# Top-2 mixture FFN behind a quantised linear block: experts chosen from token sums, and a first pair of column tiles without Strassen sums

## The reference

```python
x = x + xattn(layernorm(x), gate_up_weight, down_weight)   # per batch: int8-style linear 512 -> 512, silu(gate) * up, linear 256 -> 512
x = x + ffn(layernorm(x), gate_w, w1, b1, w2, b2)

def ffn(hidden, gate_w, w1, b1, w2, b2):                     # 8 experts, DFF = 2048
    x = hidden.reshape(-1, d)
    router_logits = x @ gate_w.T
    _, sel = top_k(router_logits.sum(axis=0), 2)             # one choice of two experts for all 2048 rows
    rw = softmax(router_logits[:, sel], axis=1)
    h = gelu(einsum('nd,kdf->knf', x, w1[sel]) + b1[sel])
    y = einsum('knf,kfd->knd', h, w2[sel]) + b2[sel]
    return einsum('nk,knd->nd', rw, y)
```

## Time and profile before

| | |
|---|---|
| median of 3 runs | 849.64 us (849.06 to 851.92) |
| the profiled execution | 847.23 us, span 845.4 us |
| TensorE | 772.4 us busy, 3569 matmuls |
| VectorE | 487.1 us, 695 instructions |
| GpSimd | 458.6 us, 463 instructions |
| ScalarE | 365.1 us, 675 instructions |
| DMA | 32.31 MB, mean 38 GB/s |

### The profile page before, as it was taken

The page is one execution under the profiler, slowest core; times in us unless marked ns, Lnnn a source line. Parts: engine busy times, 40 slices in busy tenths (PEclk is TensorE's granted clock), DMA queues, the critical chain, the costliest instruction groups (busy, mean ns, idle before and its releaser), DMA issues.

```text
span 845.4 us, 11484 instructions
## 1 busy us (share of the span) xinstructions
PE 772.4 (91%) x3569; PEld 620.1 (73%) x3575; DVE 487.1 (58%) x695; ACT 365.1 (43%) x675; POOL 458.6 (54%) x463
## 2 busy tenths in 40 slices
PE   3687766649999999999999999999999999999998
PEld 2564553337888888888888888888888888888886
DVE  2999999597545454545545454545454545454545
ACT  7975565653333343434333333333333334343422
POOL 1567779674645455555555555555454545464622
PEclk9799889869999999999999999999999999999999
DMA  8400000030101010101010101010101000000023
GB/s 340 161 2 1 1 1 1 0 98 28 50 1 50 0 50 0 50 0 50 0 50 0 50 0 50 0 50 0 50 6 43 25 25 25 25 25 25 0 88 112
DMA packets 19076, 32.31 MB, mean 38 GB/s; under 512 B 872, under 2 KB 11240, under 8 KB 18160
## 3 DMA queue, kind: packets, MB, share of 16 engines
q1 hardware_dynamic: 19056, 32.07, 10.8%
HBM read 27.87 MB, written 4.19 MB: 38 GB/s over the span
## 4 chain that ended last, share of the span: by engine, by line
PE 78%; DVE 14%; issue 3%; POOL 2%; ACT 2%; DMA 2%; SPq 0%; DVEq 0%; POOLq 0%; ACTq 0%
PE slot L739 41%; PE slot L726 35%; DVE rmax L1080 3%; DVE peak_x L1080 2%; DVE xf L1130 2%; DMA wv<-in_fside_BxS2xS 2%; DVE xo L1151 1%; DVE stats L1071 1%; DVE wv L1143 1%; DVE xf L1143 1%; DVE scale L1121 1%; DVE peak_a L1080 1%; POOL h_lo L431 1%; PE slot L603 1%; PE slot L524 0%
## 5 line engine op out<-in xcount | busy, mean ns | idle before, releaser
L726 PE MATMUL slot<-xo,a_hi 128*128 128x512 f32 x896 | 277.7, 391 | 11.5 <-DVE a_lo L1203 9.9
L1371 DVE SCALAR_TENSOR_TENSOR res<-slot,rw,res 128x512 f32<-128x512 f32 x256 | 178.6, 751 | 136.5 <-PE slot L739 136.5
L1336 DVE TENSOR_TENSOR e<-slot,e 128x512 f32<-128x512 f32 x160 | 110.6, 691 | 183.2 <-PE slot L726 183.2
L726 PEld LDWEIGHTS slot<-xo,a_hi 128*128 128x128 f32 x896 | 168.4, 189 | 47.8 <-issue 9.9
L739 PE MATMUL slot<-w_hi,h_hi 128*128 128x512 f32 x512 | 201.2, 393 | 0.5 <-POOL h_lo L431 0.5
L739 PE MATMUL slot<-w_lo,h_hi 128*128 128x512 f32 x512 | 199.4, 389 | 0.0
L739 PE MATMUL slot<-w_hi,h_lo 128*128 128x512 f32 x512 | 199.3, 389 | 0.0
L726 PE MATMUL slot<-xo,a_lo 128*128 128x512 f32 x448 | 174.9, 390 | 0.0
L431 POOL TENSOR_TENSOR h_lo<-e,h_hi 128x512 fp32r<-128x512 f32 x96 | 135.6, 1425 | 58.4 <-ACT e L984 57.3
L739 PEld LDWEIGHTS slot<-w_hi,h_hi 128*128 128x128 f32 x512 | 96.1, 188 | 25.6 <-POOL h_lo L431 6.1
L739 PEld LDWEIGHTS slot<-w_hi,h_lo 128*128 128x128 f32 x512 | 96.1, 188 | 20.2
(11 more groups left out here) (139 smaller groups left out, 787.8 us busy)
## 6 DMA issues: line engine op xcount, KB each, us to landing
raw<-in_L_ffn_w SPq DMA_DIRECT2D x32, 512.0 KB, 3.3
res<-in_x SPq DMA_DIRECT2D x4, 1024.0 KB, 9.5
wv<-in_fside_BxS2xS SPq DMA_DIRECT2D x4, 1024.0 KB, 14.8
out_x<-res SPq DMA_DIRECT2D x3, 1024.0 KB, 3.9
cv<-in_ctx SPq DMA_DIRECT2D x4, 512.0 KB, 11.0
out_x<-res SPq DMA_DIRECT2D x4, 256.0 KB, 2.7
b_row<-in_L_ffn_b SPq DMA_DIRECT2D x2, 256.0 KB, 4.9
b_rows<-in_L_ffn_b SPq DMA_DIRECT2D x1, 64.0 KB, 1.7
```

The lines of the kernel that those rows point to most:

```text
L726: last = t.matmul(dst, a[:, i, k, :], xo[tp][:, v, k, :], start=(start and n == 0), stop=(n == 3 * H - 1), skip_group_check=True)
L1336: v.tensor_tensor(dst[:, :], src, other[:, :], ALU.add).then_inc(comb_ready, 1)
L1371: v.scalar_tensor_tensor(out=r, in0=y_bank[j][:, :], scalar=rw[:, ds(p, 1), n:n + 1].rearrange("p a b -> p (a b)"), in1=r, op0=ALU.mult, o ...
```

## The change

The transposes of the second layernorm come ahead of all routers; the experts are chosen from the sum of the transposed rows over all tokens (`token_sums`, `token_total`, ScalarE's accumulating copies in `keep_full`), multiplied with the full-precision router matrix, and no longer from the logits. The routers run behind that, with both halves of the router matrix side by side as 16 columns: 16 matmuls a batch instead of 24. The first pair of column tiles uses eight plain products of 12 matmuls (`plain`, for each half of the rows) instead of seven Strassen products of 6, so it needs neither sums of weights nor sums of rows; the fourth router and the transposes of the logits stand between its products. The sums of the row blocks move from GpSimd to VectorE and behind, to be ready for the second pair. The softmax over two experts needs one power of 16 columns instead of 32. One half of the last batch's residual and normalisation moves to VectorE.

GpSimd and TensorE:

```diff
-            add_residual(3, 1)
...
-            def operand_sums(tp, router_use):
-                even, odd = 2 * tp, 2 * tp + 1
-                slot_i, n = place(router_use)
-                kept(even, 0)
-                kept(odd, 0)
-                pool.wait_ge(filled[slot_i], n + 1)
-                g.tensor_tensor(part(tp, T1L), part(tp, T1H), part(tp, T2H), ALU.subtract).then_inc(tsum_ready[tp], 1)
...
-                g.tensor_tensor(part(tp, T2L), part(tp, T3H), part(tp, T1L), ALU.subtract).then_inc(tsum_ready[tp], 1)
-                g.tensor_tensor(part(tp, T3L), part(tp, T3H), part(tp, T1H), ALU.subtract).then_inc(tsum_ready[tp], 1)
...
-                g.tensor_tensor(part(tp, T4L), part(tp, T4H), part(tp, T2L), ALU.subtract).then_inc(tsum_ready[tp], 1)
-
-            operand_sums(0, "r.1")
-            operand_sums(1, "r.3")
-
-            pool.wait_ge(lsub_ready, TOPK)
-            g.tensor_tensor(lexp[:, :, :].rearrange("p k n -> p (k n)"), euler[:, :],
-                            lsub[:, :, :].rearrange("p k n -> p (k n)"), ALU.pow).then_inc(lexp_ready, 1)
+            pool.sem_inc(sums_ready, 4)
...
-            with pool.Fori(0, PAIRS - 1) as p:
+            def first_pair():
+                hid_lo(0, 0, 0)
+                hid_lo(0, 0, 1)
+                pool.wait_ge(lsub_ready, 1)
+                g.tensor_tensor(lpow[:, :], euler[:, :], lsub[:, :], ALU.pow).then_inc(lexp_ready, 1)
+                hid_lo(0, 0, 2)
+                hid_lo(0, 0, 3)
+                weight_sums(0)
+                for i in range(4):
+                    hid_lo(0, 1, i)
+                for i in range(7):
+                    weight_lo(0, i)
+                down_lo(0, 0, 1)
+                down_lo(0, 1, 0)
+
+            first_pair()
+            with pool.Fori(1, PAIRS - 1) as p:
...
-                        for a, v in ((gwt_hi, hi), (gwt_hi, lo), (gwt_lo, hi)):
-                            last = t.matmul(ps[0:E, 0, :], a[:, H * h + k, :], xo[b // 2][:, v, k, :],
-                                            start=(n == 0), stop=(n == 3 * KD - 1))
+                        for rows_used, v in ((2 * E, hi), (E, lo)):
+                            last = t.matmul(ps[0:rows_used, 0, :], gwt[:, H * h + k, 0:rows_used],
+                                            xo[b // 2][:, v, k, :], start=(n == 0), stop=(n == 2 * KD - 1),
+                                            skip_group_check=True)
                             n += 1
...
-                pe.wait_ge(sum_ready, 1)
+                pe.wait_ge(tok_ready, 1)
                 ps, full = fill("e")
-                t.matmul(ps[:, 0, 0:E], logit_sum[:, 0:1].to_broadcast([E, P]), ident[0:E, 0:E],
-                         start=True, stop=True).then_inc(full, 1)
-
-            def logit_columns():
-                for i in range(4):
-                    pe.wait_ge(drained[i], ALL_DRAINED[i])
...
             scale_row(3, 2)
...
+            router(1)
             router(2)
-            router(3)
-            expert_sums()
-            logit_columns()
 
             def strassen(p, tp, i, dst, start, first):
                 if tp == 0:
@@ -770,8 +777,48 @@
```

```diff
 
-            pair(0, True, False)
-            with pe.Fori(1, PAIRS - 1) as p:
+            def plain(q, n):
+                f, s = TILES[n]
+                b = 2 * q + s
+                m = 0
+                for h in range(KD // H):
+                    if q == 0:
+                        pe.wait_ge(a_ops_ready, 2 * f + h + 1)
+                    pe.wait_ge(lo_ready[b], h + 1)
+                    hi, lo = HI_AT[s][h], LO_AT[s][h]
+                    for k in range(H):
+                        for a, v in ((a_hi, hi), (a_hi, lo), (a_lo, hi)):
+                            last = t.matmul(TILE_BANK[n], a[:, 2 * f + h, k, :], xo[q][:, v, k, :],
+                                            start=(m == 0), stop=(m == 3 * KD - 1))
+                            m += 1
+                last.then_inc(prod_done, 1 if n < 3 else 4)
+
+            def first_pair():
+                for tp in range(2):
+                    pe.wait_ge(hid_ready, 8 + 8 * tp)
+                    plain(tp, 0)
+                    if tp == 0:
+                        router(3)
+                    plain(tp, 1)
+                    if tp == 0:
+                        for b in range(B):
+                            logit_columns(b)
+                    plain(tp, 2)
+                    pe.wait_ge(hid_ready, 8 + 8 * tp + 2)
+                    plain(tp, 3)
+                    if tp == 0:
+                        pe.wait_ge(w2_ready, 2)
+                    down(0, tp, 0, 0, 0, True)
+                    down(0, tp, 0, 1, 1, False)
+                    last = down(0, tp, 1, 2, 1, True)
+                    if tp == 1:
+                        last.then_inc(w2_free, 1)
+                    down(0, tp, 1, 3, 0, False)
```

ScalarE and VectorE (new functions, then the order of the calls):

```diff
                 ps, empty = drain(f"y.{b}.{h}")
-                act.wait_ge(lo_ready[b], h + 1)
+                for k in range(H):
+                    ins = s.activation(part(b // 2, FULL_AT[b % 2][h])[:, k * T:(k + 1) * T], ps[:, k, :], ACT.Copy,
+                                       accum_out=tok_sum[:, H * h + k, b:b + 1])
+                ins.then_inc(empty, 1)
+
...
+                ps, empty = drain(f"y.{b}.{h}")
+                act.wait_ge(part_ready[b], 1)
                 s.copy(part(b // 2, FULL_AT[b % 2][h]), ps[:, :, :].rearrange("p k t -> p (k t)")).then_inc(empty, 1)
+
+            def keep_hi(b, h):
...
+                act.wait_ge(drained[i], n + 1)
+                s.copy(whole(b // 2, HI_AT[b % 2][h]), part(b // 2, FULL_AT[b % 2][h])).then_inc(hi_ready[b], 1)
 
             def operand_hi(tp, at, sums):
             normalise(3, 2)
-            keep_logits(1)
-            keep_block(2, 0)
-            keep_block(2, 1)
+            keep_full(2, 0)
+            keep_full(3, 0)
+            keep_summed(2, 1)
+            keep_summed(3, 1)
+            keep_hi(2, 0)
+            keep_hi(2, 1)
             keep_hi(3, 0)
             keep_hi(3, 1)
+            s.activation(gelu_warm[:, :], half[:, 0:1], ACT.Gelu_apprx_tanh)
+            keep_logits(0)
+            keep_logits(1)
+            act.sem_inc(hid_ready, 8)
+            act.sem_inc(e1_ready, 2)
+            act.wait_ge(raw1_load, 16)
+            for i in range(4):
+                plain_hi(i)
             keep_logits(2)
...
 
+            def first_pair():
+                act.wait_ge(b1_ready, 1)
+                s.copy(b1_now[:, :], b1_col[:, 0:2]).then_inc(b1_ready, 1)
+                act.wait_ge(b1_ready, 2)
+                for tp in range(2):
+                    act.wait_ge(h_ready, 4 + 4 * tp)
+                    for n in range(4):
+                        act.wait_ge(prod_done, 7 * tp + n + 1)
+                        gelu(0, n, TILES[n][0], TILE_BANK[n])
...
+                        if tp == 0 and n == 0:
+                            keep_logits(3)
+                    if tp == 0:
+                        operand_hi(0, (T2H, T2L), 4)
+                        operand_hi(0, (T3H, T3L), 4)
+                        operand_hi(0, (T1H, T1L), 4)
+                        operand_hi(0, (T4H, T4L), 4)
+                act.wait_ge(prod_done, 14)
+                act.wait_ge(sums_ready, 8)
```

```diff
+            def difference(tp, n, dst, a, c, op=ALU.subtract):
+                v.tensor_tensor(part(tp, dst), part(tp, a), part(tp, c), op).then_inc(tsum_ready[tp], 1)
+                dve.wait_ge(tsum_ready[tp], n)
+
+            def last_operands(tp):
+                difference(tp, 1, T2L, T3H, T1H)
+                difference(tp, 2, T2L, T2L, T2H, ALU.add)
+
+            def middle_operands(tp, n):
+                if n == 3:
+                    dve.wait_ge(prod_done, 7 + 7 * tp)
+                    difference(tp, 3, T1L, T1H, T2H)
+                else:
+                    difference(tp, 4, T3L, T3H, T1H)
+
+            def fourth_operand(tp):
+                v.tensor_tensor(part(tp, T4L), part(tp, T4H), part(tp, T2L), ALU.subtract).then_inc(t4_sum, 1)
+                dve.wait_ge(t4_sum, tp + 1)
...
+            def normalise_last():
+                b = B - 1
+                dve.wait_ge(nmr_ready[b], 2)
+                for j in range(H, TT):
+                    v.tensor_scalar(xv[b][:, j, :], res[:, b * TT + j, :], rstd[1][b][:, j:j + 1],
+                                    nmr[1][b][:, j:j + 1], ALU.mult, ALU.add).then_inc(xn_last, 1)
...
+            def token_sums(b):
+                ps, _ = drain(f"y.{b}.1")
+                v.tensor_reduce(tok_sum[:, H:2 * H, b], ps[:, :, :], AX.X, ALU.add).then_inc(part_ready[b], 1)
+            add_last_residual()
             moments(2, 2)
+            moments(3, 2)
+            keep_lo(0, 0)
+            normalise_last()
+            keep_lo(0, 1)
+            token_sums(2)
+            token_sums(3)
+            token_total()
             keep_lo(1, 0)
+            choose_experts()
```

(35 more changed lines are left out.)

268 lines of the change are left out of this document (133 added, 135 removed), and 8 rows, old and new, of the table SLOT_USES.

## The result

The changed kernel takes 839.88 us (median of 4 runs, 836.82 to 843.64), the kernel before, measured beside it, 849.35. The ratio is 0.988, 95% interval 0.984 to 0.993: 9.5 us faster. The prediction said 847.7 with a range from 842.0: right in sign, far too small in size, and outside its range.

The account below looks back on a forecast made before the run. TensorE, busy 91% of the span, bounds the kernel; only the stretch ahead of 226 us can change. Terms -11.2 + 3.0 + 4.2 + 0.7 + 0.4 + 1.0 = -1.9 us, from median 849.64 to 847.7 us, range 842.0 to 851.9.

Parts of the forecast that it names:

- 1 to 3, first product: Ahead of the first pair: earlier choice and side-by-side routers start the first product at 169.1 instead of 180.27 us, -11.2 us.
- 4, composition of the first pair: First pair: 192 matmuls, 43.8 us, plus fourth router and logit transposes inside, 48.7 against 45.7 us: +3.0 us.
- 5, VectorE's debt: VectorE's work before the first outputs, contending with GpSimd, makes TensorE wait mid first pair: +4.2 us, between 0.2 and 5.4.
- 6, the clock: TensorE's half clock level after the pause in the middle of the first pair: +0.7 us, between 0 and 1.7.
- 7, second half: Second half of the first pair: VectorE about level with TensorE under GpSimd's h_lo: +0.4 us, between 0 and 0.7.
- 8, second pair and on: Second pair carries late operand sums and lo subtractions that hold up h_lo: +1.0 us, between 0.5 and 1.3.
- Step 3: Routers: 16 products a batch instead of 24, three batches taking 10.9 us to 169.1, ScalarE hidden by 1.7 us.
- the choice worth nothing: Choice of experts: known near 159 us instead of 169.4, buying nothing by itself since the weights then wait for TensorE.
- Step 1: Stage ahead of the choice: two additions and half the normalisation on VectorE, last transpose at 155.6, only 0.3 us earlier.
- Rival A: First pair: VectorE on time, GpSimd yields or fits its gaps; 842.6 us, 841.4 if both additions pass; chance 0.28.
- Rival B: TensorE's pauses ahead of the routers and mid first pair cost the clock: +2.6 us, 852.2 us; chance 0.20.

Follow-up runs that it names:

- e6: Changed kernel with the expert product behind routers 0 and 1, and one lo subtraction of VectorE ahead of the choice; 844.04 us, ratio 0.993.
- e12: Changed kernel with all four routers, the expert product and the logit transposes ahead of the first pair, logits picked right after the choice; 845.96 us, ratio 0.995.
- e10: Changed kernel with the last two residual additions of batch 3 on GpSimd again, half of the normalisation staying on VectorE; 839.49 us, ratio 0.987.
- e4: Changed kernel with two GpSimd h_lo subtractions left out and its weight sums postponed, so VectorE's operand sums have SBUF to themselves; 837.33 us, ratio 0.984.
- e2: Changed kernel with VectorE's token weights and first four outputs ahead of the last three operand sums of the first half; 835.44 us, ratio 0.983.

## Why the prediction was wrong

By its own terms, in the two profiled executions, less the chance 1.4 us:

| term | predicted | measured | where |
|---|---|---|---|
| 1 to 3, first product | -11.2 | -15.9 | 162.97 - 180.27 + 1.4 |
| 4, composition of the first pair | +3.0 | +1.0 | 200 x 0.228 + 1.1 - 45.7 |
| 5, VectorE's debt | +4.2 | +3.0 | product due at 182.58, ran at 185.57 |
| 6, the clock | +0.7 | +1.7 | 0.43 a product until 189.28 |
| 7, second half | +0.4 | -0.1 | 21.76 us for 96 products at 0.228 |
| rest of the first half | | +0.2 | 29.75 us less the terms above |
| 8, second pair and on | +1.0 | +0.9 | 834.8 - 214.48 against 845.4 - 225.99 |
| sum | -1.9 | -9.2 | |

**Step 3 failed, and step 4 by the same mistake.** "A batch takes 16 products instead of 24" is wrong by a factor of two: four blocks of 128 and two matmuls for each are 8, before 12. The text ahead of the prediction has the same wrong numbers, 24 matmuls and 16, and so has the prediction's first part with its "48 router products (of 96)": they were 24 of 48. (The eight plain products, by contrast, are rightly counted: four for each half of the rows, 96 matmuls in the first pair instead of 84.) Of the 10.9 us for three routers 5.7 were left, of the 3.6 for the fourth 1.8. Count and view were both at hand: the trace of before has

```profile
L603 PE MATMUL slot<-xo,gwt_hi x32: 390/473/737, 125.5 to 166.6; 128*8 128x512 f32 x32
...
L603 PE MATMUL slot<-xo,gwt_lo x16: 387/398/632, 126.5 to 166.9; 128*8 128x512 f32 x16
```

that is 48 in four batches. A count from the loops should be held against the xcount of its group before a duration is multiplied with it.

**The mistake hid the gate.** With routers of 10.9 us, ScalarE's chain seemed covered by 1.7 us, and the choice worth nothing. With 5.7 us both are the wrong way round: ScalarE's copies and the arrival of the weights end last, TensorE idles 1.23 us for them, and each microsecond of a later choice costs nearly one at the first product (e6: 2.9 for 3.45; e12: 7.4 for 7.65). The step says "if that cover went, the first product would be late by what exceeds it": this is what happened. A second size was off beside it: ScalarE's work from the first hi copy to the last weight copy took 7.6 us as summed, but I had it end at 167.4, and it ended at 162.02 + 1.32 = 163.34, or 164.7 with the chance 1.4 added. With the right count and this error the step would still have said 167.5. Of the 5.2 us of the right count, the gate of 1.2 went off again, and the routers started 0.8 sooner than forecast (156.03 + 1.4 = 157.4 instead of 158.2): that is, within 0.1, the 4.7 by which terms 1 to 3 were wrong.

**Step 1** read the direction right and missed that the step as made is not the best one: the two additions cost VectorE more on the path than they save GpSimd (e10).

**Step 5 was right in mechanism**, place and partner, and 1.2 us too large. The power did not get in between, h_lo did twice (4.43 for two sums, where 2.48 is their own length), and a weight sum slowed the token weights. e4 shows that without those collisions there is no wait at all, e2 that the order on VectorE decides whether they matter. The Trainium skill (SBUF — State Buffer, Who interferes with whom) says that a VectorE instruction with two SBUF inputs contends with a GpSimd instruction that reads SBUF, and that the ports the two engines share are an exclusive lock. For h_lo the trace agrees: two of each alternate in 4.4 us. For the power (2.90 us on 16 columns, 174.03 to 176.93) it does not: the two sums beside it (174.15 to 176.64) took 2.49 us, their own length, and the power ran beside them (as far as GpSimd's spans can be read). If anyone was held up there, it was the power: on 4 columns it took 1.02 us where VectorE had no sum, and 1.91 beside a subtraction of VectorE that kept its own length. GpSimd's and VectorE's timelines after:

```profile
147.95 1.91 POOL L327 TENSOR_TENSOR rstd<-var_e,neg_half 128x4 f32<-128x4 f32 x1 [1.76 <-DVE var_e L1151]
```

```profile
147.78 1.22 DVE L1225 TENSOR_TENSOR xo<-xf,xo 128x1024 fp32r<-128x1024 f32 x1
```

So the strict reading of that rule (5.4 us) was further from the 3.0 measured than the 4.2 that I took.

**Step 6** was too small. Each of the seven profiled pauses of 2.4 to 2.8 us for that output was followed by the half level, and its price in the changed kernel's profile was 1.7, the upper bound.

**Rival A** (842.6, 841.4 with both additions passing) came nearest in its number, by luck: its mechanism, a VectorE on time, didn't occur, and pause and clock cost 4.7 us. **Rival B**'s condition was not reached, though the half level behind the short pause, which it needed, does occur.

What stays open: the share of the plain products. No run has the early choice with Strassen products. e12 against before leaves some 3 us to plain products, shorter router, moved sums and an arrival of the weights that is up to 2.3 us earlier behind the last transpose, together; the one term that the rows price is 12 more products, 2.7 us, against 6.2 us that lay between the arrival of the weights and the first product before (landed by 174.08, first product 180.27) and 1.0 in e12 (172.23 to 173.26).

## What to carry to other kernels

Hold each count that is multiplied against the xcount of its group in the trace: a factor of two in a resource that seems to bound a stage turns every "hidden behind it" of that stage round. Where one transfer depends on one decision, look for what else, linear in the same data, could decide earlier; an earlier decision gains until other work covers the transfer. And in a queue written by hand, put what releases the bottleneck's buffers ahead of what is only needed a stage later: moving three large sums behind four outputs gave 4.4 us.
